# Lags of a channel loaded in one run with two-lag sums on VectorE, and another issue order of loads in the dense stage

## What is computed

```python
# 1: one causal convolution per channel, its 1024 lags k[c] made from the parameters
u = x * mask                                   # steps below the batch's length
x = x + (fft_conv(u, k) + u * D[:, None]) * mask
# 2: a 64x64 matrix for each batch, out of 16
x = x + einsum('bct,bcd->bdt', x, W1[cond])
# 3: dense 1024 -> 1024, bias, and a rank-16 adapter for each batch, out of 32
x = x + x @ W2.T + bias + (x @ A2[i].T) @ B2[i].T
# 4: dense 1024 -> 1024 and a rank-32 adapter, A out of 5
x = x + x @ W3.T + 0.5 * (x @ A3[j]) @ B3.T
```

## Time and profile before

| | before |
|---|---|
| median of three runs | 1584.57 us (1582.99 to 1592.93) |
| the profiled execution | 1583.27 us |
| its span, first to last instruction | 1581.1 us |
| TensorE (PE) busy | 94% of the span |
| VectorE (DVE) busy | 68% |
| ScalarE (ACT) busy | 40% |
| GpSimd (POOL) busy | 7% |
| mean granted clock | 0.988 |

### The profile page before, as it was taken

How to read it: one execution, slowest core, us unless ns; L and a number is a source line. 1 busy time by engine, 2 the same in 40 slices (tenths; PEclk the granted TensorE clock), 3 DMA queues, 4 the chain that set the end, 5 groups by cost and what they waited for, 6 DMA issues and landing times.

```text
span 1581.1 us, 33465 instructions
## 1 busy us (share of the span) xinstructions
PE 1487.6 (94%) x10701; PEld 1422.1 (90%) x10701; DVE 1073.5 (68%) x2203; ACT 635.6 (40%) x1185; POOL 116.0 (7%) x197
## 2 busy tenths in 40 slices
PE   6999999999999996999999999999999999999998
PEld 5888888999989895999999999999999999999988
DVE  7955376676766674676676776677677677677674
ACT  3331256565666652243243243233243233333332
POOL 3551210000000000000000000000000000000000
PEclk9999999999999996999999999999999999999999
DMA  9724289899999986345445445545545545545642
GB/s 244 108 103 114 46 254 294 280 291 298 291 292 286 295 255 209 126 147 178 154 146 180 153 145 174 160 127 185 163 126 186 153 138 162 177 139 159 180 140 74
DMA packets 183699, 289.73 MB, mean 183 GB/s; under 512 B 64065, under 2 KB 120781, under 8 KB 181009
## 3 DMA queue, kind: packets, MB, share of 16 engines
q1 hardware_dynamic: 173436, 254.72, 53.8%
q10 hardware_dynamic: 10230, 34.59, 6.4%
HBM read 214.09 MB, written 75.15 MB: 183 GB/s over the span
## 4 chain that ended last, share of the span: by engine, by line
PE 34%; DMA 9%; SPq 9%; issue 6%; DVE 4%; DVEq 0%; ACT 0%
PE ps L1554 11%; PE ps L1555 11%; DMA x_in<-x_d 8%; PE ps L1525 6%; SPq L1223 5%; SPq L1222 3%; DVE late L1385 2%; PE ps L1564 2%; PE ps L1562 2%; PE ps L1536 1%; PE ps L1531 1%; DVE hrow L1444 1%; DVE hrow L1440 1%; DMA x_nat<-in_x 0%; DVE x_in L1390 0%
## 5 line engine op out<-in xcount | busy, mean ns | idle before, releaser
L1554 PE MATMUL ps<-weights,xs 128*128 128x256 f32 x1536 | 397.4, 289 | 0.0
L1555 PE MATMUL ps<-weights,xs 128*128 128x256 f32 (+1 forms) x1536 | 388.9, 292 | 0.0
L1554 PE MATMUL ps<-weights,xa 128*128 128x352 f32 (+1 forms) x1152 | 331.5, 315 | 4.4 <-DVE weights L1416 1.3
L1555 PE MATMUL ps<-weights,xa 128*128 128x256 f32 (+1 forms) x1152 | 325.5, 297 | 0.0
L1554 PEld LDWEIGHTS ps<-weights,xs 128*128 128x128 f32 x1536 | 292.6, 190 | 0.0
L1555 PEld LDWEIGHTS ps<-weights,xs 128*128 128x128 f32 x1536 | 292.5, 190 | 0.0
L1304 ACT ACTIVATE a<-ps 128x512 f32<-128x512 f32 x128 | 76.6, 599 | 396.6 <-PE ps L1525 396.6
L1554 PEld LDWEIGHTS ps<-weights,xa 128*128 128x128 f32 x1152 | 220.6, 192 | 9.6 <-issue 9.6
L1097 PE MATMUL ps<-toep,ut 128*128 128x512 f32 (+2 forms) x1152 | 227.6, 342 | 0.0
L1555 PEld LDWEIGHTS ps<-weights,xa 128*128 128x128 f32 x1152 | 219.2, 190 | 0.0
L1097 PEld LDWEIGHTS ps<-toep,ut 128*128 128x128 f32 x1152 | 195.0, 189 | 16.8
(11 more groups left out here) (221 smaller groups left out, 2095.6 us busy)
## 6 DMA issues: line engine op xcount, KB each, us to landing
xt<-in_xt SPq DMA_DIRECT2D x64, 512.0 KB, 6.8
x_d<-yo SPq DMA_DIRECT2D x64, 512.0 KB, 4.0
x_in<-x_d SPq DMA_DIRECT2D x64, 512.0 KB, 4.8
x_nat<-in_x SPq DMA_DIRECT2D x64, 512.0 KB, 3.9
out<-y_out ACTq DMA_DIRECT2D x64, 512.0 KB, 4.3
toep_raw<-kern_d SPq DMA_DIRECT2D x64, 384.0 KB, 5.0
toep_raw<-fold_d SPq DMA_DIRECT2D x64, 320.0 KB, 6.3
stack<-b_d SPq DMA_DIRECT2D x130, 128.0 KB, 3.6
```

The source lines that it names most:

```text
L1554: mm(left[0], x_part, left[1], start=first and is_wide, stop=end, skip_group_check=True)
L1555: ins = mm(right[0], x_part, right[1], start=first and is_wide and H_AT[m] > 0, stop=end, skip_group_check=True)
```

## The change

In the weight stage `fold_in`, `fold_sum` and `fold_d` go, with their two transfers and the sum. In the convolution stage all 1024 lags of a channel come in one load, `lags`, three channels ahead into four buffers; VectorE makes the 640 two-lag sums of a channel itself, in `fold` (one buffer). `toep` is split in two pieces on both engines, 768 columns from `lags` and 640 from `fold`. `ut` is split over 7 of 8 blocks of 128 columns (`SPLIT`); the eighth was and is used unsplit. `udiff` and the sum are made two channels ahead (`sums`). `yo` has two buffers in place of four. SP waits for the last `b2` store before the channel loop, since `b2_last` and later buffers share memory.

In the dense stage the stack loads of pair n are issued in pair n, behind the loads of `x1_in` of pair n+1, in place of the end of pair n-1. `late` becomes 512 columns of 16 bits in place of 1024 of 8, one half at a time, so `choose` waits until the predicated copy before has read it. The loads of `x_nat` stay where they were.

```diff
+    xt, lags, yo = [None] * BUFS, [None] * BUFS, [None] * 2
+    lags[0], o = at("lags0", [P, T], F32, o_rest)
+    fold, o = at("fold", [P, TFOLD], F32, o)
+    xt[0], o = at("xt0", [P, K8, P], F32, o)
+    assert o <= o_part + 4 * 4 * C
...
+    for i in range(1, 3):
+        lags[i], o = at(f"lags{i}", [P, T], F32, o)
+    xt[2], o = at("xt2", [P, K8, P], F32, o)
     shared_in, o = at("shared_in", [P, QT], F32, o)
+    yo[1], o = at("yo1", [P, T], F32, o)
     b2_last, _ = at("b2_last", [P, 2, T], F32R, o)
-    for i in (2, 3, 1):
-        yo[i], o = at(f"yo{i}", [P, T], F32, o)
-    assert o <= o_st + 2 * 8 * T + 1536
+    lags[3], o = at("lags3", [P, T], F32, o)
+    xt[3], o = at("xt3", [P, K8, P], F32, o)
+    assert o <= o_rest
...
-    late = place("late", [P, T], U8)
+    late = place("late", [P, HB], U16)
...
+    toep_view = bass.AP(tensor=kern_d.tensor, offset=0, ap=[[T + P, C], [1, P], [1, T]])
...
-            sp.wait_ge(kern_stored, 32)
-            sp.dma_start(fold_in[:], kern_d[:, 0:T]).then_inc(in_fold, 16)
...
-            sp.wait_ge(fold_ready, 1)
-            sp.dma_start(fold_d, fold_sum[:]).then_inc(fold_stored, 16)
...
-            def load_toep(k, u):
+            def load_lags(k, u):
                 h = UNROLL * k + u
-                ready(sp, toep_hi, h - 1)
-                ready(sp, toep_lo, h - 1)
-                raw, landed = toep_raw[u % 2], toep_in[u % 2]
-                sp.dma_start(raw[:, TFOLD:], toep_view[bass.ds(h, 1), :, :].squeeze(0)).then_inc(landed, 16)
-                sp.dma_start(raw[:, 0:TFOLD], fold_view[bass.ds(h, 1), :, :].squeeze(0)).then_inc(landed, 16)
+                ready(sp, tri_ready, h - BUFS + 1)
+                ready(sp, toep_lo, h - BUFS + 1)
+                sp.dma_start(lags[u % BUFS][:], toep_view[bass.ds(h, 1), :, :].squeeze(0)).then_inc(lags_in[u % BUFS], 16)
...
-            load_toep(0, 0)
+            load_lags(0, 0)
             load_x(0, 0)
...
-            load_toep(0, 1)
+            load_lags(0, 1)
+            load_lags(0, 2)
             load_x(0, 2)
             sp.wait_ge(job_free, freed("b2_3"))
             sp.dma_start(b2_rows[3 * P:4 * P], f(b2_last[:])).then_inc(b2_stored, 16)
+            sp.wait_ge(b2_stored, 16 * (AR // P))
...
-                if loads or u < UNROLL - 2:
-                    load_toep(k + (u + 2) // UNROLL, (u + 2) % UNROLL)
                 if loads or u < UNROLL - AHEAD:
+                    load_lags(k + (u + AHEAD) // UNROLL, (u + AHEAD) % UNROLL)
...
-                copy(ut[u % 2][:, 0], xt[u % BUFS][:], ACT.Copy).then_inc(ut_hi, 1)
-                act.wait_ge(toep_in[u % 2], toep_count(k, u) + 32)
-                copy(toep[u % 2][:, 0], toep_raw[u % 2][:, ::-1], ACT.Copy).then_inc(toep_hi, 1)
-                copy(tri[u % 2][:], toep_raw[u % 2][:, :TOEP + TFOLD - P - 1:-1], ACT.Copy).then_inc(tri_ready, 1)
+                copy(ut[u % 2][:, 0, 0:SPLIT], xt[u % BUFS][:, 0:SPLIT], ACT.Copy).then_inc(ut_hi, 1)
+                act.wait_ge(lags_in[u % BUFS], count_in(k, u) + 16)
+                copy(toep[u % 2][:, 0, 0:TOEP], lags[u % BUFS][:, :T - TOEP - 1:-1], ACT.Copy)
+                act.wait_ge(fold_ready, h + 1)
+                copy(toep[u % 2][:, 0, TOEP:], fold[:, ::-1], ACT.Copy).then_inc(toep_hi, 1)
                 act.wait_ge(diff_ready, h + 1)
                 copy(dt[u % 2][:, 0], udiff[:], ACT.Copy).then_inc(dt_hi, 1)
+                copy(tri[u % 2][:], lags[u % BUFS][:, :T - P - 1:-1], ACT.Copy).then_inc(tri_ready, 1)
...
-            dve.wait_ge(in_fold, 16)
-            tt(fold_sum[:], fold_in[:, 0:FW], fold_in[:, QT:QT + FW], ALU.add).then_inc(fold_ready, 1)
...
+            def sums(k, u):
+
+                dve.wait_ge(lags_in[u % BUFS], count_in(k, u) + 16)
+                ready(dve, toep_lo, UNROLL * k + u)
+                tt(fold[:], lags[u % BUFS][:, 0:TFOLD], lags[u % BUFS][:, QT:QT + TFOLD], ALU.add).then_inc(fold_ready, 1)
+                dve.wait_ge(x_in[u % BUFS], count_in(k, u) + 16)
+                ready(dve, dt_lo, UNROLL * k + u)
+                raw = xt[u % BUFS]
+                tt(udiff[:], raw[:, 0:2], raw[:, 2:4], ALU.subtract).then_inc(diff_ready, 1)
+
             def split_low(k, u):
                 h = UNROLL * k + u
-                dve.wait_ge(x_in[u % BUFS], x_count(k, u) + 16)
-                ready(dve, dt_lo, h)
-                raw = xt[u % BUFS]
-                tt(udiff[:], raw[:, 0:2], raw[:, 2:4], ALU.subtract).then_inc(diff_ready, 1)
                 dve.wait_ge(ut_hi, h + 1)
-                tt(ut[u % 2][:, 1], raw[:], f(ut[u % 2][:, 0]), ALU.subtract).then_inc(ut_lo, 1)
+                tt(ut[u % 2][:, 1, 0:SPLIT], xt[u % BUFS][:, 0:SPLIT], f(ut[u % 2][:, 0, 0:SPLIT]), ALU.subtract).then_inc(ut_lo, 1)
                 dve.wait_ge(toep_hi, h + 1)
-                tt(toep[u % 2][:, 1], toep_raw[u % 2][:, ::-1], f(toep[u % 2][:, 0]), ALU.subtract).then_inc(toep_lo, 1)
+                tt(toep[u % 2][:, 1, 0:TOEP], lags[u % BUFS][:, :T - TOEP - 1:-1], f(toep[u % 2][:, 0, 0:TOEP]), ALU.subtract)
+                dve.wait_ge(fold_ready, h + 1)
+                tt(toep[u % 2][:, 1, TOEP:], fold[:, ::-1], f(toep[u % 2][:, 0, TOEP:]), ALU.subtract).then_inc(toep_lo, 1)
                 dve.wait_ge(dt_hi, h + 1)
                 tt(dt[u % 2][:, 1], udiff[:], f(dt[u % 2][:, 0]), ALU.subtract).then_inc(dt_lo, 1)
...
-            def channel(k, u, ahead=True):
-                if ahead:
+            def channel(k, u, ahead=2):
+                if ahead > 0:
                     split_low(k + (u + 1) // UNROLL, (u + 1) % UNROLL)
+                if ahead > 1:
+                    sums(k + (u + 2) // UNROLL, (u + 2) % UNROLL)
                 back(k, u)
 
             dve.wait_ge(p3_part, 1)
+            sums(0, 0)
             split_low(0, 0)
             b2_low(3, b2_last)
+            sums(0, 1)
...
+            def stacks(n):
+
+                if isinstance(n, int) and n == 0:
+                    return
+                sp.wait_ge(p_done, n)
+                for v in range(2):
+                    load_stack(v, ids(sp, n, v, B))
+
             def pair(n, last_one):
+                sp.wait_ge(mixed, 4 * n + 4)
                 if last_one:
+                    stacks(n)
                     return
-                sp.wait_ge(mixed, 4 * n + 4)
                 for v in range(2):
                     load_x1(n + 1, v)
+                stacks(n)
                 a, l = [ids(sp, n + 1, v, B) for v in range(2)], [ids(sp, n + 1, v, 2 * B) for v in range(2)]
                 for v in range(2):
                     sp.wait_ge(h_lo[v], n + 1)
@@ -1257,9 +1261,6 @@
                     for v in range(2):
                         sp.wait_ge(chosen[v], 2 * n + 4)
                         load_x(n + 2, v)
-                sp.wait_ge(p_done, n + 1)
-                for v in range(2):
-                    load_stack(v, a[v])
...
+                if half == 1:
+                    dve.wait_ge(chosen[v], 2 * n + 1)
+                elif v == 1:
+                    dve.wait_ge(chosen[0], 2 * n + 2)
+                else:
+                    ready(dve, chosen[1], 2 * n)
                 for q in range(2 * half, 2 * half + 2):
-                    cols = slice(q * QT, (q + 1) * QT)
-                    nc.vector.tensor_scalar(late[:, cols], ramp[:], float(q * QT), lens_cols[:, bass.ds(2 * n + v, 1)],
+                    nc.vector.tensor_scalar(late[:, q % 2 * QT:q % 2 * QT + QT], ramp[:], float(q * QT), lens_cols[:, bass.ds(2 * n + v, 1)],
                                             ALU.add, ALU.is_ge).then_inc(late_made, 1)
                 dve.wait_ge(late_made, 8 * n + 4 * v + 2 * half + 2)
                 dve.sem_inc(choice_begun, 1)
                 cols = slice(half * HB, (half + 1) * HB)
-                nc.vector.copy_predicated(x1_in[v][:, cols], late[:, cols], x_nat[v][:, cols]).then_inc(chosen[v], 1)
+                nc.vector.copy_predicated(x1_in[v][:, cols], late[:], x_nat[v][:, cols]).then_inc(chosen[v], 1)
```

More of the change, by code:

```diff
@@ L31 @@
 TFOLD = 3 * QT - P
-FW = TOEP
+SPLIT = K8 - 1
 LAYOUT_END = 229368
@@ L656, in front @@
                 copy(shared_in[:], ps[1][:, (u % 2) * HB:(u % 2) * HB + QT], ACT.Copy).then_inc(shared_out, 1)
-                ready(act, x1_stored[u % BUFS], x_count(k, u))
-                if isinstance(k, int) and k == 0 and u in (2, 3):
-                    act.wait_ge(b2_stored, 16 * (AR // P))
-                copy(yo[u % BUFS][:, 0:HB], ps[2 + u % 2][:, 0:HB], ACT.Copy).then_inc(y_front, 1)
+                ready(act, x1_stored[u % 2], count_in(k, u, 2))
+                copy(yo[u % 2][:, 0:HB], ps[2 + u % 2][:, 0:HB], ACT.Copy).then_inc(y_front, 1)
             def channel(k, u, ahead=True):
@@ L955, in _ @@
             for u in range(UNROLL):
-                channel(GROUPS - 1, u, ahead=u < UNROLL - 1)
+                channel(GROUPS - 1, u, ahead=UNROLL - 1 - u)
         @block.tensor
```

50 lines of the change are left out of this document (16 added, 34 removed).

## The result

| | before | after |
|---|---|---|
| median on the same chip | 1583.78 us (1578.46 to 1592.93) | 1518.86 us (1515.54 to 1520.33) |
| the profiled execution, its span | 1583.27, 1581.1 us | 1520.33, 1518.6 us |

The ratio is 0.9581, with a 95% interval of 0.9534 to 0.9629: faster, as forecast, by 10 us more than the 1529 forecast. Of the 10 us, 7.8 lie between the profiled executions (1528.1 worked out, 1520.33 measured). The rest is scatter: the profiled execution of after was the slowest of its four, and the prediction had put the median above the profile.

The account below looks back on a forecast made before the run. TensorE was taken as the bound, only its idle time winnable. 1583.27 - 18.3 (convolution) - 37.7 (dense) + 0.85 (start) = 1528.1, with the median 1.3 above the profiled execution: 1529 us, range 1519 to 1548.

Parts of the forecast that it names:

- Convolution, -18.3: Steady convolution: ScalarE's load wait before `toep` goes; 62 channels at 5.79 us, 359.0 for 377.32, so -18.3 us.
- the floor of the working (356.5): Steady convolution: 62 channels at an unbroken 5.75 us are 356.5 us, so it can give 20.8 at most.
- VectorE just fits: Convolution channel: VectorE gets 0.84 us more, 5.06 busy, 87% of 5.79, ending `udiff` at 5.7 with `back` wanted at 5.75.
- The first rival: Convolution half won: VectorE at 87% or late bursts of loads leave 5.95 us a channel; gain 8.4, 1539 us; chance 0.18.
- The `b2` store, 0: Before the channel loop: SP's wait for the last store holds the fourth lags about 4 us, 8.6 allowed: 0.
- The start, +0.85: Channel 0: VectorE's chain to `dt` low now holds the sum, split and shorter `ut`: +0.85 us, bounds 0 and +2.
- Dense, -37.7: Dense stage: `x_in` issued ahead of the stacks ends `turn`'s wait for `hrow`: -37.7 us over 30 pairs.
- the 7.6 of pair 0: Dense, pair 0: `x_in` issued behind 1 MB of natural rows, VectorE went on 7.6 us later; even that hides the landing.
- the company: Dense stage: the `x_in` loads now lie beside the output stores and share the DMA engines; the sum stays the same.
- The tables: Dense stage: they go out about 3.4 us later; VectorE waits 0.6, TensorE 0, bound +0.5 us a pair.
- a floor of 40.9: Dense stage: thirty pairs at the last whole pair's 28.59 us are 857.7, so it can give 40.9 us at most.
- nearer the waits: Dense stage: -37.7 taken between recorded waits, 36.3, and floor, 40.9, since one pair or another will be hit by something else.

Follow-up runs that it names:

- the kernel with three: Changed kernel with the two-lag sum of each channel made twice more on VectorE, into a place nobody reads: 1541.09 us, ratio 0.9712.
- the kernel with the order alone: Kernel of before with only SP's new issue order in the dense stage, `late` still in 8 bits: 1539.84 us, ratio 0.9710.
- the two repairs: Changed kernel, last `b2` store ahead of the third channel's loads, first two natural rows ahead of the last convolution-store wait: 1519.17 us.
- the kernels with two and three sums: Changed kernel with the two-lag sum made once more (two sums), 1518.48 us, or twice more (three sums), 1541.09 us.

## Why the prediction was right, and where not

**The bound, and the direction.** Right. TensorE's idle time was all there was to win. By the page's totals, span less busy, it fell from 93.5 us to 47.2, and the busy time fell too, by 16.2, though TensorE ran the same 10701 matmuls: a part of what a wait costs is drawn as work (the group of six takes 0.95 behind a wait, 0.88 without, and the last 0.16 us of the row ahead of a wait are part of it), and 1.6 us are the lower clock in before. Together they are the 62.5 us of the span.

**Convolution, -18.3: measured -19.3.** The way was right in each step. The later load is gone and with it ScalarE's wait of the earlier trace rows: over channels 1 to 63 there is one wait of ScalarE for `lags`, 2.1 us. Without the wait at channel 3, as in the kernel with the new convolution alone, the 62 channels are 356.7, the floor of the working (356.5). VectorE's operations came out as the slope had them, mean ns of each from 214 to 574.5 us (forecast 1089, 955 and 821):

```profile
L915 DVE TENSOR_TENSOR ut<-xt,ut 128x896 fp32r<-128x896 f32 x62 | 67.7, 1092 | 16.7 <-ACT ut L629 16.7
L917 DVE TENSOR_TENSOR toep<-lags,toep 128x768 fp32r<-128x768 f32 x62 | 59.4, 959 | 16.3 <-ACT toep L633 16.3
...
L906 DVE TENSOR_TENSOR fold<-lags 128x640 f32<-128x640 f32 x62 | 50.7, 818 | 0.0
```

The Trainium skill (VectorE: DVE Perf Modes, The TRN2 errata) gives a float32 sum of two tensors of N columns as (N + 151) / 0.96 ns. An estimate by that formula is 1091, 957 and 824; the rows agree within 1%. VectorE is busy for 305.49 / 62 = 4.93 us a channel, forecast 5.06: the working added whole durations, but two operations in a row overlap by some 0.09 us in the records (406.36 + 0.82 against 407.09), and there are two more junctions. The added waits on its own semaphores exposed nothing: the start-to-start steps behind `dt` and behind the sum, 0.34 and 0.73, are also those of the extra sums in the kernel with three (400.25, 400.59, 401.32), which wait for nobody. So the channel ran unbroken at 5.75, not at the 5.79 taken; "VectorE just fits" was too careful, since 1.08 us are free. The first rival, convolution half won through a full VectorE, falls with that, and the room where it would begin to be true is now known.

**The `b2` store, 0.** Wrong by about a microsecond here. Its landing was taken as 4 us; SP was held for 6.6 (SP's issues of after, then VectorE):

```profile
209.99 0.35 SPq L395 DMA_DIRECT2D b_d<-b_last  x1
216.90 0.33 SPq L375 DMA_DIRECT2D lags<-kern_d  x1
217.26 1.94 SPq L369 DMA_DIRECT2D xt<-in_xt  x1
```

```profile
221.00 0.83 DVE L906 TENSOR_TENSOR fold<-lags 128x640 f32<-128x640 f32 x1
224.50 0.43 DVE L910 TENSOR_TENSOR udiff<-xt 128x256 f32<-128x256 f32 x1 [2.67 <-DMA xt<-in_xt]
```

On VectorE the sum, at 221.00, did not wait for the lags. What the step forgot is the `xt` load queued behind them, which `udiff` wants just behind the sum: VectorE sat 2.67 us, and TensorE 1.11 at 229.13. The same wait was 2.44 us in the kernel with `x_in` between the stacks and absent in the one with the new convolution alone, so the term is 0 to 2.5.

**The start, +0.85.** Not seen as such. VectorE's chain for channel 0, first split to `dt` low, did grow, by 0.7 us, but the four weight sums ahead of it took 5.88 us where before they took 6.91, and channel 0 waited 2.32 us instead of the earlier trace rows's 2.68. Why those sums were quicker is open. Channel 0 began 1.26 us later, but the kernels here with the old convolution began it at 207.7 to 209.3 and those with the new at 207.2 to 209.8 (the kernel with the new convolution alone last of all), so nothing can be read from it.

**Dense, -37.7: measured -44.5.** The mechanism was right. In one pair of after, SP's issues and then VectorE:

```profile
1090.75 0.86 SPq L1201 DMA_DIRECT2D x_in<-x_d  x2
1095.71 0.34 SPq L1216 DMA_DIRECT2D stack<-b_d  x1
...
1106.25 0.36 SPq L1190 DMA_DIRECT2D tab<-a_d  x1
```

```profile
1096.97 0.69 DVE L1484 TENSOR_TENSOR xs<-s,xs 128x512 fp32r<-128x512 f32 x1 [1.52 <-ACT xs L1342]
1097.58 0.47 DVE L1391 TENSOR_SCALAR late<-ramp,lens_cols 128x256 uint16<-128x256 int16 x2
...
1100.87 0.42 DVE L1446 COPY hrow<-ps 64x48 f32<-64x48 f32 x2 [0.50 <-PE ps L1561]
...
1112.05 0.63 DVE L1413 TENSOR_TENSOR tab<-tab 128x128 f32<-128x128 f32 x2 [1.47 <-DMA tab<-a_d]
```

`late` waits for nothing; where the earlier trace rows had VectorE late for TensorE, it now waits 0.50 for TensorE before `hrow`. The rows landed 6.1 us after issue where the earlier trace rows has 4.8, between that row and the 7.6 of pair 0, and were in time. That is also what the rule cited in the prediction (the Trainium skill, DMA: Bandwidth & Descriptors, Queues, rings and completion order) would have; with the page's issue rows of after:

```profile
x_in<-x_d SPq DMA_DIRECT2D x64, 512.0 KB, 6.1
...
out<-y_out ACTq DMA_DIRECT2D x64, 512.0 KB, 5.4
```

The other queue paid too: the output stores land in 5.4 us, 4.3 before. ScalarE waits longer for them, 45.9 us in 30 pieces before L1340 and 58.9 before L1345 over the stage, where it was 13.9 and 1.6 us, and hands 1.52 on to VectorE in the row above. Before the second of these it had waited 53.6 us for TensorE in before, so most of that wait only changed its owner. The prediction named the company but not who would wait in it; it stayed hidden with 0.5 us to spare before `hrow`. The tables were mis-sized too, all but harmlessly: the first goes out 15.5 us behind the issue of `x_in`, by the working 14.6 (1204.9 against 1190.3), and VectorE waited 39.0 us for them in 29 pieces, 1.3 a pair for 0.6. The way from the `x_in` issues to the first stack load, with two id reads in it, took 4.1 us (1091.61 to 1095.71), not 1.4. TensorE never waited for `weights` at a pair's start. But in pair 1 VectorE's wait for `tab` was 3.34 us (658.11); the sums and then ScalarE's `y_out` (662.26) came late behind it, and TensorE waited 1.12 us (662.89). That pair took 29.64 us.

**The step that failed** is the price of a wait, and the floor with it. Between the recorded waits, 36.3, and a floor of 40.9 the prediction went "nearer the waits", as if a wait cost what its row records. The kernel with `x_in` between the stacks shows 0.22 us more for each, 6.4 us over 30 pairs. The floor was too high as well. The last whole pair, 28.59 us, was read as a pair without a break because no wait stands at its end. But at its start stands a `turn` that had waited, which is 0.06 us: in the three other kernels that wait before `turn`, this pair is 28.45 or 28.46. The other 0.13 is the longer kind of pair, which has nothing to do with a wait. Pairs with no wait at either end, of which before had none, take 28.40. Thirty of these are 852.0, so the stage could give 46.6, not 40.9, and 44.5 of it came; the rest is in four pairs of after that are 0.1 to 1.2 us longer.

The 30 waited pairs of before, less their recorded waits, exceed 28.40 by 10.3 us together. Twelve of them are 28.60 to 28.63, seventeen 28.70 to 28.76 and one 30.19. That is 6.4 us for the waits, 2.3 for the longer kind and 1.6 for the lower clock in pair 20. The last two, 3.9 us of the 44.5, belong to the one execution that was profiled and not to the order of the loads. The 6.4 could be seen in before: a matmul's row there also ends 0.16 us behind the start of the next, and 28.61 less 0.22 is 28.39. The low end of the range stood on the same floor; with 46.6 in it the range would have begun at 1513.

**The convolution's floor** had been read with the care that the dense one lacked: two channels, one with a restart in it and one without, 5.85 and 5.75. The pair had only one reading, and it was of the longer kind.

## What to carry to other kernels

A floor read from a trace must come from several stretches that are unbroken at both ends; one that begins right behind a wait still holds its restart, and equal stretches can come in two lengths. Where an engine waits once per iteration, price the wait at its record, plus the overlap of two rows that follow each other without a wait, plus the later start of what comes behind it. Look at the granted clock of each odd iteration by itself: a mean of 1.00 over the stage hid a fall of 3.4 us. A load that stands ahead of work for which the next load waits makes a loop; its lead, not its size, decides, so see first what each wait in the loop is queued behind, and count the transfers queued behind a delayed one as well.

## What was not expected of the hardware

- A wait of TensorE before `turn` costs 0.22 us more than the idle time that its row records, in every kernel here that has it (28.60 to 28.63 against 28.40 in pairs of the shorter kind). In a channel it is 0.23: in after the channel that ends with the wait is 5.91 without the recorded 1.11, the one behind it 5.82, and one without a wait 5.75. On VectorE it is some 0.1 a wait.
- SP's two id reads between `x_in` and the first stack load took 4.1 us in after and in the kernel with the order alone. Two others, between the stacks of the two tiles, took 1.5, and so did those right behind `x_in` where `x_in` stood between the stacks. So the two loads ahead of them are not what holds them up; what does is open.
- Eight of the ten kernels have one or two pairs that are 1.2 to 3.4 us longer than the others. Six of these pairs, in before and in the kernels with the convolution alone (two), with `late` alone (two) and with the two repairs, hold one stretch of 3.4 us at the lower clock level (granted 0.50). Each such stretch begins 0.1 to 1.5 us behind a wait of TensorE of 1.8 to 2.05 us, and where it could be told apart it cost 1.6 us. Other waits as long had none behind them (1.9 and 2.0 us in the kernel with `late` alone). In after and in the other kernels with its dense stage the long pair is pair 1, with one wait of 1.1 to 1.9 us for `y_out`.
- In the kernels with two and three sums and in that with lags two ahead most dense pairs are 28.53, not 28.40, though their dense stage is that of after. Seventeen pairs of before have the same 0.13 us. What decides between the two lengths is open; it moves no verdict.
- Nearly the same mask, written as 16 bits rather than 8, took 281 ns in place of 345; at the end of the kernel the runs show nothing of it.
